# Cross attentions on one Trainium2 core: scores and transposes issued by pairs of heads in place of one by one

## The reference

```
x = _layernorm(x + _L0_xattn_ref(x, ctx_1024, ctx_1024, mask_1x1xSxS2_if1, L0_xattn_W_q, ...))
x = _layernorm(x + _L1_xattn_ref(x, ctx_1024, mask_BxS2_bf1, L1_xattn_W_q, L1_xattn_b_q, ...))

q = to_heads(x @ W_q + b_q)                  # [16, 16 heads, 112, 16]
k, v = to_heads(ctx @ W_kv + b_kv)           # [16, 16 heads, 375, 16]
A = softmax(q @ k.T / 4 + mask)              # [16, 16 heads, 112, 375]
y = (A @ v).reshape(16, 112, 256) @ W_o + b_o
```

## Time and profile before

| | us |
|---|---|
| time, median of 3 runs | 2751.66 (2748.56 to 2760.43) |
| the profiled execution's own time | 2747.25 |
| its span, first to last instruction | 2745.5 |
| PE busy | 2404.7 (88%) |
| DVE busy | 1716.1 (63%) |
| ACT busy | 1335.1 (49%) |
| cross0 at full flow, 165 to 525 us: PE busy | 334.90 of 360, granted clock 0.99 |
| cross1 at full flow, 1411 to 1775 us: PE busy | 338.61 of 364, granted clock 0.99 |
| mean granted TensorE clock | 0.944 |

### The profile page before, as it was taken

One profiled execution on the slowest core, in us unless ns is written; L12 is line 12 of the kernel. 1 busy time (PEld: TensorE's weight loads), 2 busy tenths in 40 slices (PEclk: granted clock), 3 DMA queues, 4 the chain that ended last, 5 costly groups with the idle time before them and its releaser, 6 DMA issues. The chain is left out here.

```text
span 2745.5 us, 49497 instructions
## 1 busy us (share of the span) xinstructions
PE 2404.7 (88%) x15015; PEld 1865.5 (68%) x15015; DVE 1716.1 (63%) x4359; ACT 1335.1 (49%) x3569; POOL 521.4 (19%) x623
## 2 busy tenths in 40 slices
PE   7589999878999964888869999869999999999995
PEld 5467777557999953555557777657777777777772
DVE  2346667544676634666647766645776766777668
ACT  2156766533454522555446666645444444444430
POOL 3100000040000023000010000035443433344331
PEclk9789999888999985999989999879999999999998
DMA  4066655221344421000065566210100101001000
GB/s 146 12 148 126 122 124 124 59 83 62 126 133 154 127 68 48 1 0 0 0 156 123 122 122 123 58 47 25 35 16 21 35 1 36 16 20 36 1 1 27
DMA packets 185552, 184.28 MB, mean 67 GB/s; under 512 B 54929, under 2 KB 178978, under 8 KB 185378
## 3 DMA queue, kind: packets, MB, share of 16 engines
q1 hardware_dynamic: 182306, 174.80, 25.6%
q0 software_dynamic: 3072, 7.34, 0.9%
HBM read 130.93 MB, written 51.18 MB: 66 GB/s over the span
## 5 line engine op out<-in xcount | busy, mean ns | idle before, releaser
L800 ACT ACTIVATE cross_pr<-cross_sc,cross_mn 112x375 f32<-112x375 f32 x512 | 310.5, 607 | 230.3 <-DVE cross_mn L890 228.3
L2252 ACT ACTIVATE switch_vt<-switch_ps,switch_chosen 112x128 f32<-112x128 f32 x1024 | 290.3, 368 | 267.4 <-PE switch_ps L104 256.9
L2326 DVE SCALAR_TENSOR_TENSOR all_x<-switch_ps,switch_go,all_x 112x256 f32<-112x256 f32 x512 | 245.8, 480 | 220.2 <-PE switch_ps L104 213.6
L890 DVE CUSTOM_DVE_ANT_0 cross_sc<-cross_ps,cross_masked 112x375 f32<-112x375 f32 x512 | 273.2, 544 | 175.1 <-PE cross_ps L688 153.9
L696 PE MATMUL cross_ps<-all_ident,cross_pr 112*125 112x112 f32 x1536 | 257.0, 276 | 22.3 <-DVE cross_pt L897 21.2
L696 PEld LDWEIGHTS cross_ps<-all_ident,cross_pr 112*125 112x125 f32 x1536 | 234.1, 190 | 44.3 <-DVE cross_pt L897 27.8
L2117 POOL TENSOR_TENSOR switch_v_halves<-switch_vt 112x512 f32<-112x512 f32 x128 | 164.6, 1286 | 485.7 <-ACT switch_vt L2252 485.6
L2326 DVE SCALAR_TENSOR_TENSOR switchgates_x_odd<-switch_ps,switch_go,switchgates_x_odd 112x256 f32<-112x256 f32 x512 | 243.6, 476 | 0.0
L688 PE MATMUL cross_ps<-cross_k,cross_q 96*112 96x376 f32 x512 | 222.0, 434 | 13.4 <-DMA cross_k<-cross_k_dram 10.3
L102 PE MATMUL switch_ps<-switch_ow,switch_cth 128*112 128x512 f32 x512 | 208.7, 408 | 12.8 <-DVE switchgates_x_odd L2326 12.4
L102 PE MATMUL switch_ps<-switch_vw,switchgates_xh 128*112 128x512 f32 x512 | 208.2, 407 | 7.9 <-DVE switch_vw L2311 7.9
(11 more groups left out here) (353 smaller groups left out, 5347.4 us busy)
## 6 DMA issues: line engine op xcount, KB each, us to landing
cross_k<-cross_k_dram SPq DMA_DIRECT2D x96, 375.0 KB, 8.0
experts_w_raw<-in_L_ffn_w_dram SPq DMA_DIRECT2D x30, 1024.0 KB, 5.6
cross_k_dram<-cross_ks SPq DMA_DIRECT2D x32, 750.0 KB
cross_cx_raw<-in_ctx_dram SPq DMA_DIRECT2D x32, 375.0 KB
cross_q<-cross_q_dram SPq DMA_DIRECT2D x192, 56.0 KB
switch_raw<-in_L_ffn_v_w_dram SPq DMA_DIRECT2D x16, 512.0 KB
switch_raw<-in_L_ffn_o_w_dram SPq DMA_DIRECT2D x8, 1024.0 KB
cross_q_dram<-cross_qs SPq DMA_DIRECT2D x32, 224.0 KB, 3.2
```

The source lines that it names most:

```text
L800: nc.scalar.activation(pr[:, h % NB, :], sc[:, h % NB, :], ACT.Exp, bias=mn[parity][:, h:h + 1], scale=-1.0, accum_out=rs[parity][:, h:h + ...
L890: nc.vector.tensor_tensor_reduce(out=sc[:, h % NB, :], in0=ps[0:T, SCORES + h % 2, 0:S2], in1=mask_of[:], scale=-0.25, scalar=3e38, op0=AL ...
L2252: last = nc.scalar.activation(vt[:, b % 2, n * EH + e, :], ps[0:T, VALUES + n, e * PW:(e + 1) * PW], ACT.Copy, scale=chosen[parity][:, b, ...
L2326: nc.vector.scalar_tensor_tensor(out=total[:, b, :], in0=ps[0:T, OUTPUTS + n % 2, i * D:(i + 1) * D], scalar=go[:, b, e:e + 1], in1=total[ ...
```

## The change

PE's loop over single heads becomes a loop over pairs. For steps p and p+1 PE issues both scores, then both turns, and then what else belonged to step p and step p+1, in the old order. No instruction is added or dropped and no wait is edited; ACT, DVE, POOL and SP keep their order.

```diff
             def batch(b, parity, kind):
                 first, units = kind == "first", units_of(kind)
-                for i in range(H):
-                    scores(b, parity, i)
-                    if i >= TL:
-                        turn(b, i - TL)
-                    elif not first:
-                        turn(b - 1, i - TL + H)
-                    if FRONT_AT.get(i) in units:
-                        u = FRONT_AT[i]
-                        front(b + 1, 1 - parity if u in (V0, V1, V2) else parity, u)
-                    if not first and i in TAIL_AT:
-                        tail(b - 1, TAIL_AT[i])
-                    if i in VALUES_AT:
-                        values(b, parity, VALUES_AT[i])
-                    elif i in VALUES_OF_LAST and not first:
-                        values(b - 1, 1 - parity, VALUES_OF_LAST[i])
+                for pair in range(0, H, 2):
+                    for i in (pair, pair + 1):
+                        scores(b, parity, i)
+                    for i in (pair, pair + 1):
+                        if i >= TL:
+                            turn(b, i - TL)
+                        elif not first:
+                            turn(b - 1, i - TL + H)
+                    for i in (pair, pair + 1):
+                        if FRONT_AT.get(i) in units:
+                            u = FRONT_AT[i]
+                            front(b + 1, 1 - parity if u in (V0, V1, V2) else parity, u)
+                        if not first and i in TAIL_AT:
+                            tail(b - 1, TAIL_AT[i])
+                        if i in VALUES_AT:
+                            values(b, parity, VALUES_AT[i])
+                        elif i in VALUES_OF_LAST and not first:
+                            values(b - 1, 1 - parity, VALUES_OF_LAST[i])
```

## The result

The change makes the kernel slower: 2789.27 us (median of 4, 2787.06 to 2791.44) against 2750.11 (median of 4), a ratio of 1.0139 with a 95% interval of 1.0106 to 1.0172. A second set, taken later, in which the kernel before takes 2726.42, gave 1.0155 (1.0139 to 1.0170). The forecast was 2801, range 2763 to 2832. The profiled execution took 2787.06 us, 39.8 more than that of before. From the first scores to the last tail part 3 the two cross attentions take 397.0 and 395.7 us, before 376.4 and 376.8: +39.5 together, so all but 0.3 us of the loss is in them.

The account below looks back on a forecast made before the run. PE was taken to set the pace, with short stalls waiting for DVE. The profiled 2747.25 us plus 31 (26 x 1.3 - 3, mainly the stall at T(10)) plus 22 for the clock gave 2801 us, range 2763 to 2832.

Parts of the forecast that it names:

- The stall at T(10): PE waits for DVE's evacuate(8) 2.15 us in place of 0.59; cost 1.3 us a batch, bounds 0.3 to 2.1.
- The rest of the batch: S(14) to the next S(10), 16.61 us: gains and losses sum to +0.05, taken as 0, within -0.8 to +0.8.
- Spacing: On PE, S S 0.20 and T T 0.32 us make a pair 1.08 in place of 1.05, 0.03 more.
- The rival of cheaper dense work: S S at 0.12 and T T at 0.25 give back 25 us, about 2758, within 0.5%; chance 0.11.
- Its upper bound for S S: Second score up to 0.53 us after the first, costing 0.3 us a pair where PE is not stalled anyway.
- Batches 0, 14 and 15: Batch 0 has no tail, so 0; batches 14 and 15 gain 0.8 us each, four times, -3 in all.
- The clock: Low clock of 3.4 us after T(10)'s stall costs 1.2 us in 7 of 10 batches: +22 us, bounds 0 and 44.
- the case that was given 0.50: Stall at T(10) with clock falls: own range 2785 to 2830 us, chance 0.50.
- the one of the stall alone: Rival: stall at T(10) but no clock fall, 2778 us, range 2768 to 2788; chance 0.28.
- The faster rival: evacuate(8) ready when PE is, so T(10) costs nothing: -1.2 us a batch, -31, 2716 us; chance 0.06.

Follow-up runs that it names:

- steps 12 and 13 single: Changed kernel with steps 12 and 13 back in the old one-head-at-a-time order, other pairs kept: 2757.78 us, 1.0051.
- that pair alone: Kernel before with only steps 12 and 13 paired: 2794.88 us, 1.0174.
- evacuate(8) early: Changed kernel with DVE doing evacuate(8) straight after maximum(11), before Q and the tail: 2746.56 us, 0.9991.
- the filler run: Changed kernel with the 12 matmuls of values(1) issued two extra times ahead of turn(10): 2784.29 us, 1.0129.
- The same edit: DVE does evacuate(i-3) straight after maximum(i) at steps 5 to 15: 1.0056 on the kernel before, 0.9704 on the changed kernel.
- both edits: Changed kernel with other work between a pair's two turns and DVE's early evacuations at steps 5 to 15: 2705.09 us, 0.9930.

## Why the prediction was right, and where a size was off

- **The stall at T(10).** Worked out: T(10) at 5.73 after S(10), a stall of 2.15, S(14) at 8.33. Measured 5.75, 2.24 counted the same way (2.09 of it idle), 8.24. The chain had the measured lengths (DVE's Q 2.89 after S(10), reckoned 2.87). S(14) comes 0.09 early because a stalled turn takes 0.41 to the next other work, reckoned 0.52. Tail part 2 was put at 2.05, where the earlier trace rows give 2.23; it came at 1.97, off the path. The runs with steps 12 and 13 single, with that pair alone, and with evacuate(8) early show that this wait is the cause.
- **The rest of the batch.** Taken as unchanged, 16.61 us; measured 16.69. The sum was right and its items less so. The gains at V2, C1 and part 1 came, and T(12) is 0.64 late (0.7 reckoned). T(14) stands idle for 0.86, before for 0.06 and 0.45 by turns, which is more than the +0.2 reckoned. T(6) comes 0.28 late (0.5 reckoned), and T(4) 0.35, which I had not seen.
- **Spacing.** S S taken as 0.20, measured 0.19 (0.60 for two less 0.41 for one); T T taken as 0.32, measured 0.33 (0.81 less 0.48). The rival of cheaper dense work falls: nothing is won by it. Its upper bound for S S, 0.3 a pair, should have read 0.36.
- **Batches 0, 14 and 15.** In batches 14 and 15, S(10) to S(14) takes 5.28 in place of 6.02 wherever the clock stays up, so the -0.8 is there; with the rest of these batches it is -4.2 in all, reckoned -3. Two things were not reckoned. Batch 0, put at 0 since it has no tail, has the stall as well: Q alone is enough to keep evacuate(8) back (T(10) idle for 1.15 us; 6.41 from S(10) to S(14) in place of 5.03). And 5.4 us came back behind the last scores, where before ran at a granted clock of 0.54 in cross0 and the changed kernel at 1.00.
- **The clock.** Falls behind T(10) are there, the size was off: 22 us reckoned, some 8 measured (8.6 batch by batch, 7.6 by the filler run). The 7 batches in 10 and the 1.2 us were the author's estimate, with one fall in coupled attention as the only measured case. It falls in 4 of 10 full batches, not 7, and costs 0.9, not 1.2, since in such a batch T(12) no longer waits (none marked in the batch from 376.07, 0.49 us in the next): that stall covers part of it. Where it can't, with steps 12 and 13 alone paired, most falls cost 1.6. This term is why the forecast stood 12 us above the result.
- **How much of the number is luck.** Without the clock the forecast had +31 (26 x 1.3 - 3), and the trace has +31. That this fits to a microsecond is luck: the 26 periods lose 35.8, not 33.8, the start 4.7 more, and the end gives back 9.6 where 3 was reckoned, 5.4 of it in a stretch that ran at another clock. The time, 2789.27, lies between the case that was given 0.50 (2785 to 2830) and the one of the stall alone (up to 2788): at the lower edge of the first, as the clock does fall but costs little.
- **The faster rival** named the right lever: evacuate(8) ready when PE is. It was bounded as if DVE's order were fixed; the run with evacuate(8) early reached before, not 31 us less, because T(12) was next.

## What to carry to other kernels

When engines that work off their streams in order pass buffers around (K0 stood behind T(10) here through 2.09 us of idle time), work placed in front of a waiting instruction is cover, and regrouping a queue for tidier runs of one kind moves that cover behind the wait; look for the longest chain on the engine that frees the buffer, and count what the waiting engine has left to do before it. The same edit can lose in one order (1.0056) and win in another (0.9704). After taking a wait away, ask which instruction is next in line for the same engine. A consumer moved to the front of its queue helps only if its producer comes early too (0.9930 for both edits, 0.9704 for one).

## What the runs showed of the hardware that was not expected

The clock's falls were fewer and cheaper than one stall of 2.09 us in every batch suggested: 5 in 13 full batches of each cross attention, in both sets of the changed kernel, each 3.4 us at half clock, and 0.77 to 1.04 us of time each in the first. With a wait of 1.36 us at T(12) and none at T(10) there were some, too: 7 falls in 26 with steps 12 and 13 single, 2 in 26 with evacuate(8) early. With 1.36 us of matmuls put into the stall there was none, although 0.80 us of idle time stayed before T(10), and more later in the batch.
